# Shared experts as a loop with four scattered tiles per sequence, and the last three sequences in the head of the next stage

## The reference, cut to what matters

```
x = x + norm(attention(norm(x)))
x = x + norm(moe0(norm(x)))      # 16 experts, inner width 176, top 2, and shared experts of inner width 352
x = x + norm(ssm(norm(x)))       # a state space scan
x = x + norm(moe1(norm(x)))      # 16 experts, inner width 128, top 8, and shared ones of 256
```

```
y = sum over the two: w_e * ((silu(t @ w1[e].T) * (t @ w3[e].T)) @ w2[e].T)
z = (silu(t @ sw1.T) * (t @ sw3.T)) @ sw2.T      # the shared experts, for every token
moe0 = y + z
```

## Time and profile before

| | |
|---|---|
| median of 3 runs | 1998.63 us |
| profiled execution | 1997.82 us, its span 1996.1 us |
| PE busy | 1867.9 us, 94% of the span |
| PEld busy | 1413.5 us, 71% |
| DVE busy | 1270.9 us, 64% |
| ACT busy | 763.9 us, 38% |
| POOL busy | 426.5 us, 21% |
| mean granted clock | 0.959 |

### The profile page before, as it was taken

How to read it: one execution, slowest core, us unless ns; L and a number is a source line. 1 busy time by engine, 2 the same in 40 slices (tenths; PEclk the granted TensorE clock), 3 DMA queues, 4 the chain that set the end, 5 groups by cost and what they waited for, 6 DMA issues and landing times.

```text
span 1996.1 us, 34048 instructions
## 1 busy us (share of the span) xinstructions
PE 1867.9 (94%) x10114; PEld 1413.5 (71%) x10115; DVE 1270.9 (64%) x3685; ACT 763.9 (38%) x1479; POOL 426.5 (21%) x712
## 2 busy tenths in 40 slices
PE   5999999979989999568999999999999999999998
PEld 3566666557766666346888788888878887888787
DVE  3677776536422222387777877787787778877743
ACT  1566666632223333242343333334333433433321
POOL 1243444323744444200110011001001100110000
PEclk8999999979989999677999999999999999999999
DMA  9900000001322323411101110110111011101110
GB/s 359 211 4 1 0 0 1 1 1 64 116 93 93 95 92 95 184 35 59 59 6 64 62 61 5 64 58 19 51 64 59 6 64 59 54 15 48 43 48 11
DMA packets 75230, 121.03 MB, mean 61 GB/s; under 512 B 18164, under 2 KB 59252, under 8 KB 74612
## 3 DMA queue, kind: packets, MB, share of 16 engines
q1 hardware_dynamic: 68212, 100.92, 15.9%
q0 software_dynamic: 6912, 18.92, 2.7%
HBM read 81.73 MB, written 38.08 MB: 60 GB/s over the span
## 4 chain that ended last, share of the span: by engine, by line
PE 42%; issue 39%; DVE 9%; POOL 7%; ACT 2%; DMA 1%; DVEq 0%; SPq 0%; POOLq 0%; ACTq 0%
PE bank L599 5%; PE bank L184 5%; PE bank L1151 4%; PE bank L620 4%; PE bank L1216 3%; POOL sorted_in L822 2%; PE bank L1109 2%; PE bank L193 2%; PE bank L1157 2%; PE bank L1139 2%; PE bank L1244 2%; PE bank L610 1%; PE bank L528 1%; PE bank L1704 1%; DVE comb_got L2089 1%
## 5 line engine op out<-in xcount | busy, mean ns | idle before, releaser
L184 PE MATMUL bank<-moe_xT,up_w 128*128 128x256 f32 x2304 | 552.3, 383 | 0.0
L184 PEld LDWEIGHTS bank<-moe_xT,up_w 128*128 128x128 f32 x2304 | 433.9, 190 | 69.7 <-issue 11.4
L227 ACT ACTIVATE moe_silu<-bank 128x256 f32<-128x256 f32 x288 | 110.7, 384 | 609.2 <-PE bank L184 609.2
L193 PE MATMUL bank<-down_w,moe_hT 128*128 128x256 f32 x1152 | 305.4, 388 | 3.6 <-ACT moe_y L230 2.1
L193 PEld LDWEIGHTS bank<-down_w,moe_hT 128*128 128x128 f32 x1152 | 206.0, 190 | 37.9 <-issue 7.6
L1390 DVE TENSOR_REDUCE q_slots<-bank 128x4 f32<-128x1024 f32 (+1 forms) x96 | 117.7, 1226 | 77.0 <-PE bank L1151 76.4
L1298 ACT ACTIVATE probs<-bank 128x1024 f32<-128x1024 f32 x96 | 98.2, 1023 | 99.4 <-PE bank L1157 99.4
L599 PE MATMUL bank<-up_w,moe_xT 128*128 x320 | 116.7, 488 | 0.7 <-ACT moe_xT L663 0.6
L794 DVE TENSOR_TENSOR moe_h<-moe_silu,bank 128x176 f32<-128x176 f32 x80 | 27.0, 338 | 138.6 <-issue 86.2
L326 POOL TENSOR_TENSOR moe_prstd<-moe_pmv,minus_half 128x2 f32<-128x2 f32 x16 | 11.0, 690 | 484.4 <-DVE moe_pmv L304 484.4
L1151 PE MATMUL bank<-kT,qT 16*128 16x256 f32 (+1 forms) x1024 | 114.4, 351 | 0.0
(11 more groups left out here) (296 smaller groups left out, 3233.0 us busy)
## 6 DMA issues: line engine op xcount, KB each, us to landing
up_w<-comb_rows SPq DMA_DIRECT2D x32, 768.0 KB, 5.3
comb_got<-results SPq DMA_DIRECT2D x16, 768.0 KB, 7.8
moe_rows<-sorted_in SPq DMA_DIRECT2D x80, 128.5 KB
sorted_in<-zero SPq DMA_DIRECT2D x10, 1024.0 KB, 10.3
down_w<-comb_rows SPq DMA_DIRECT2D x16, 512.0 KB, 7.2
up_w<-in_up SPq DMA_DIRECT2D x2, 3168.0 KB, 15.3
up_w<-in_up SPq DMA_DIRECT2D x2, 2304.0 KB, 11.9
results<-moe_s_y SPq DMA_DIRECT2D x16, 256.0 KB
```

Source lines behind the costliest of these rows:

```text
L184: last = mm(k.bank[:, UP_BANK + i % 3, half * S:(half + 1) * S], m.w_up[:, c, at + half * m.inter:at + (half + 1) * m.inter], m.xT[:, par, ...
L193: last = mm(k.bank[:, SUM_BANK, j * D:(j + 1) * D], m.hT[:, i % 3, j * P:(j + 1) * P], m.w_down[:, m.expert(i), :], start=(i == 0 and j == ...
L227: nc.scalar.activation(m.silu[:, i % 3, :], k.bank[:, UP_BANK + i % 3, 0:S], ACT.Silu).then_inc(m.silu_ready, 1)
```

## The change

Three parts, by the code alone:

1. `SharedSteps` takes the place of `shared_steps`. It has 13 sequences (`EARLY`): five in the head, three turns of two in a loop, two in the rest. Sequences 4 to 11 carry four `scatter` steps each, two behind the first chunk and one behind each other (`PAIR_ROWS` = 4 buffers of pairs). `choose` 14 comes last but for one `down`.
2. POOL's scatter takes the places straight from DVE's tile; its copy and its spare add are gone. POOL's list is not a loop: 32 calls in a row.
3. Sequences 13, 14 and 15 of the shared experts (`Late`) come in the head of the fused loop, with the tiles and banks of moe1 (bank 7 for the transpose and for `down`, banks 4 to 6 for `up`) and one y buffer. `l_end`, behind period 0, waits for their stores.

```diff
-CHOICE = {..., (4, 0): (14,)}
+CHOICE = {...}
+PAIR_ROWS = 4
+EARLY = 13
+LAST_CHOICE = 14
...
+class SharedSteps:
+    def __init__(self, chunks):
+        self.chunks = chunks
+        self.turns = (EARLY - 3 - SCATTERS_FROM) // 2
+    def sequence(self, t, par, scatters, last):
+        ready = 0
+        for c in range(self.chunks):
+            yield "up", t, par, c
+            if c == 0 and (not isinstance(t, int) or t > 0):
+                yield "down", t - 1, (par - 1) % 2, 0
...
+            if c == 0 and not last:
+                yield "norm", t + 1, (par + 1) % 2, 0
+            if c == 1 and not last:
+                yield "turn_x", t + 1, (par + 1) % 2, 0
...
+            while scatters and ready < -(-PAIR_ROWS * (c + 1) // self.chunks):
+                yield "scatter", (t - SCATTERS_FROM) * PAIR_ROWS + ready, 0, ready
+                ready += 1
...
+    def rest(self):
+        yield from self.sequence(EARLY - 2, (EARLY - 2) % 2, True, False)
+        yield from self.sequence(EARLY - 1, (EARLY - 1) % 2, False, True)
+        yield "choose", LAST_CHOICE, 0, 0
+        yield "down", EARLY - 1, (EARLY - 1) % 2, 0
...
         if what == "scatter":
-            par = t % 2
-            if begun(t - 1):
-                dve.wait_ge(m.scattered[par], (t - par) * 16)
+            if begun(t - c):
+                dve.wait_ge(m.scattered[c], 8 * (t - c))
             for j in range(2):
-                normalise(m.pairs[:, par, j, 0:D], t)
+                normalise(m.pairs[:, c, j, 0:D], t)
...
-            pool.wait_ge(m.rows_ready, t + 1)
-            chain.link(g.tensor_copy(m.place[:, 2 * par:2 * par + 2], cols(m.places, t, 2)))
-            g.tensor_tensor(k.pool_spare[:, 0:1], k.minus_half[:, 0:1], k.minus_half[:, 0:1], ALU.add)
...
+    def scatter(t):
+        row = t % PAIR_ROWS
+        pool.wait_ge(m.rows_ready, t + 1)
+        for j in range(2):
+            at = bass.IndirectOffsetOnAxis(m.places[:, 2 * t + j:2 * t + j + 1], 0)
+            g.indirect_dma_start(m.sorted_in, at, m.pairs[:, row, j, :], None).then_inc(m.scattered[row], 16)
+    for t in range(TILES):
+        scatter(t)
...
+def late_tensor(k, m, pe):
...
+        if what == "l_turn":
+            pe.wait_ge(s.xn_ready, t + 1)
+            pe.wait_ge(s.y_read, t)
...
+        if what == "l_up":
+            w, lo = s.wide(c), E * 2 * s.inter + c * P
+            pe.wait_ge(s.xT_ready, m.turns + n + 1)
+            if n > 0:
+                pe.wait_ge(s.h_ready, m.up(t - 1, c) + 1)
...
+        if what == "l_down":
+            pe.wait_ge(s.h_ready, m.up(t + 1, 0))
...
+def late_scalar(k, m, act):
...
+        if what == "l_down":
+            act.wait_ge(s.y_full, m.turns + n + 1)
+            if n > 0:
+                act.wait_ge(s.stored[(t - 1) % 2], 16 * ((t - 1) // 2 + 1))
+            nc.scalar.copy(moe.y[:].rearrange("p j d -> p (j d)"), k.bank[:, SUM_BANK, :]).then_inc(s.y_read, 1)
...
     def head(self):
+        a, b, c = range(EARLY, B)
+        yield "c_fetch", 0, 0, 0
+        for what, t, i in (("l_norm", a, 0), ("l_turn", a, 0), ("l_up", a, 0), ("c_sum", 0, 0), ("l_up", a, 1), ("c_sum", 0, 1),
+                           ("l_up", a, 2), ("l_h", a, 0), ("c_norm", 0, 0), ("l_h", a, 1), ("c_fetch", 1, 0),
+                           ("experts", 0, 0), ("norm", 0, 0), ("l_h", a, 2), ("l_norm", b, 0), ("norm", 0, 1),
+                           ("l_down", a, 0), ("turn_x", 0, 0), ("l_turn", b, 0), ("feat", 0, 0), ("l_up", b, 0), ("feat", 0, 1),
+                           ("l_h", b, 0), ("l_up", b, 1), ("bcdt", 0, 0), ("l_h", b, 1), ("l_up", b, 2), ("turn_dt", 0, 0),
+                           ("dt", 0, 0), ("table", 0, 0), ("conv", 0, 0), ("one_plus", 0, 0), ("l_h", b, 2), ("table", 0, 1),
+                           ("dt", 0, 1), ("conv", 0, 1), ("l_norm", c, 0), ("dt", 0, 2), ("table", 0, 2), ("l_down", b, 0),
+                           ("gate", 0, 0), ("conv", 0, 2), ("l_turn", c, 0), ("gate", 0, 1), ("conv", 0, 3), ("l_up", c, 0),
+                           ("silu", 0, 0), ("l_up", c, 1), ("c_sum", 1, 0), ("l_h", c, 0), ("l_up", c, 2), ("c_sum", 1, 1),
+                           ("l_h", c, 1), ("c_norm", 1, 0), ("turn_c", 0, 0), ("turn_c", 0, 1), ("l_h", c, 2),
+                           ("norm", 1, 0), ("norm", 1, 1), ("turn_x", 1, 0), ("l_down", c, 0), ("dt", 0, 3), ("turn_dA", 0, 0),
+                           ("xdt", 0, 0)):
+            yield what, t, t % 2, i
+        yield from self.period(0, 0)
+        yield "l_end", B, 0, 0
+        yield from self.period(1, 1)
```

More of the change, by code:

```diff
@@ L388 @@
 CHOICE = {(0, 0): (0,), (0, 1): (1,), (0, 2): (2, 3), (1, 0): (4, 5), (1, 1): (6,), (1, 2): (7,), (2, 1): (8,), (2, 2): (9, 10),
-          (3, 0): (11,), (3, 1): (12,), (3, 2): (13,), (4, 0): (14,)}
+          (3, 0): (11,), (3, 1): (12,), (3, 2): (13,)}
 RANKS = {2: 0, 3: 1}
 SCATTERS_FROM = 4
[L394 to L415, removed]
+PAIR_ROWS = 4
@@ L529, in turn, with shared @@
         last.then_inc(done, 1)
-    def shared(what, t, c):
+    def shared(what, t, par, c):
         if what == "turn_x":
@@ L565, in shared @@
                              stop=True).then_inc(m.ranks_full, 1)
[L567 to L570 removed]
+    go_through(m.shared, pe, shared)
+    pe.wait_ge(m.y_read, EARLY)
     pe.wait_ge(m.table_ready, 1)
@@ L652, in shared @@
             nc.scalar.activation(m.score, m.score, ACT.Exp).then_inc(m.exp_ready, 1)
-    for what in shared_steps(m.shared_chunks):
-        shared(*what)
+    go_through(m.shared, act, shared)
     def block(what, b, row):
@@ new lines, in late_vector, with step @@
+def late_vector(k, m, dve):
+    s, moe = m.sparse, m.moe
+    def step(what, t, par, c):
+        n = t - EARLY
+        if what == "l_norm":
+            if n > 0:
+                dve.wait_ge(s.xT_full, m.turns + n)
+            for j in range(SEQ_TILES):
+                last = normalised(k, moe.xn[:, j, :], SEQ_TILES * t + j)
+            last.then_inc(s.xn_ready, 1)
+        if what == "l_h":
+            w = s.wide(c)
+            dve.wait_ge(s.silu_ready, m.up(t, c) + 1)
+            if n > 0:
+                dve.wait_ge(s.y_full, m.turns + n)
+            k.nc.vector.tensor_tensor(moe.hT[0:w, c, :], moe.silu[0:w, c, :], k.bank[0:w, UP_BANK + c, S:2 * S],
+                                      ALU.mult).then_inc(s.h_ready, 1)
+    return step
@@ L873, with late_sync, step @@
+def late_sync(k, m, sp):
+    s, moe = m.sparse, m.moe
+    def step(what, t, par, c):
+        if what == "l_down":
+            sp.wait_ge(s.y_read, t + 1)
+            sp.dma_start(s.shared_rows(t), moe.y[:]).then_inc(s.stored[t % 2], 16)
+        if what == "l_end":
+            for stored in s.stored:
+                sp.wait_ge(stored, 16 * B // 2)
+    return step
 HEADS, KV = 16, 4
@@ L2196, in head @@
[L2196 to L2199, removed]
-        for what, i in (("norm", 0), ("norm", 1), ("turn_x", 0)):
-            yield what, 1, 1, i
-        for what in ("dt", "turn_dA", "xdt"):
-            yield what, 0, 0, 3 if what == "dt" else 0
-        for t in (0, 1):
-            yield from self.period(t, t % 2)
+        a, b, c = range(EARLY, B)
+        yield "c_fetch", 0, 0, 0
```

162 lines of the change are left out of this document (105 added, 57 removed).

## The result

The change makes the kernel slower, by less than 1%: 2015.01 us (median of 9 runs, 2004.32 to 2020.05) against 1998.63 (9 runs, 1994.6 to 2004.96), ratio 1.0071, 95% interval 1.0049 to 1.0093. The forecast was 1986.5, and its range ended at 1998. Single times of either kernel spread over 10 to 16 us, so I compare stages within the profiled executions first, and times by their ratios.

The account below looks back on a forecast made before the run. TensorE, busy 94% of the span, was taken as the bound. Span 1996.1 - 22.5 (shared stage) + 11 (fused loop's head) = 1984.6 us; with the offset to measured time, 1986.5 us; range 1978 to 1998.

Parts of the forecast that it names:

- POOL's pace: Shared stage: a tile's two indirect DMAs take 2.56 us instead of 2.92, so 32 tiles take 82 us.
- wait price of 0.03: Shared stage: 0.03 us more per tile for waiting directly ahead of an indirect DMA, lowering the gain from 23.4 to 22.5 us.
- POOL no faster: Rival, shared stage: the gap between waiting DMAs stays as long as with copy and add; gain 11.9, time 1997.7; chance 0.13.
- The sum of the stage: Shared stage: three sequences fewer and quicker POOL tiles bring the first fetch of sorted rows earlier, -22.5 us.
- Clock through the scatter loop at 1.00: Shared stage: TensorE's clock stays 1.00 despite one gap of about 1.8 us in 10.
- Scatter loop loses clock: Rival, shared stage: TensorE at half clock needs 17 us a sequence; two such cost 10 us, time 1997; chance 0.04.
- Head +11: Head of the fused loop: three late sequences delay the first dab by 11 us, own spread +8 to +18.
- Cold head: Rival, fused loop's head: clock stays at 1.2 GHz from 826 on, head costs +34 us, time 2009.6; chance 0.06.
- hidden head: Rival, fused loop's head: late steps cost only DVE's and ACT's additions, 4 us or less, time 1979.5; chance 0.13.
- store behind the expert loads: Rival, fused loop's head: first late store lands about 6 us late, holding ACT's second y copy; time 1992; chance 0.08.
- Steady part: Fused loop after the first dab: equal time to the end in both kernels, difference 0.
- the upper end of the head: Fused loop's head: with the clock at half throughout, the first dab comes at 902.5 instead of 868.2, +34 us.

Follow-up runs that it names:

- e2_straight: Changed kernel with the shared experts' stage written out straight, without the loop, on TensorE, ACT, DVE and SP; 2010.93 us, ratio 1.0049.
- e12: e2_straight with indirect DMAs writing 256 of 257 columns (1,024 bytes a row) to a tensor of their own, experts' part left out; 1989.81 us, ratio 0.9942.
- e10: e2_straight with indirect DMAs writing 64 of 257 columns (256 bytes a row) to a tensor of their own, experts' part left out; 1989.38 us, ratio 0.9940.
- e13: e2_straight with indirect DMAs writing 128 of 257 columns (512 bytes a row) to a tensor of their own, experts' part left out; 1990.58 us, ratio 0.9958.
- e1: Changed kernel with POOL's offset copy and spare add put back ahead of each tile's two indirect DMAs, loop kept; 2006.34 us, ratio 1.0032.
- e4: Changed kernel with POOL's copy and spare add put back and the shared stage written out straight; 2003.37 us, ratio 1.0016.
- e5: e2_straight with POOL's 64 indirect DMAs replaced by 64 plain ones from SP to consecutive rows, experts' result wrong; 1979.0 us, ratio 0.9893.
- e14: e2_straight with POOL's 64 indirect DMAs replaced by 64 plain ones from POOL itself to consecutive places, experts' result wrong; 1979.2 us, ratio 0.9899.
- e9: e2_straight with two small POOL copies behind every indirect DMA, spacing the same 64 DMAs at 2.0 us; 2038.74 us, ratio 1.0191.

## Why the prediction was wrong, point by point

- **POOL's pace**: right inside a row of DMAs, 2.53 us a tile against 2.56; no wait price of 0.03 showed, and *POOL no faster* falls. But the 64 DMAs took 101.1 us (481.62 to 582.70) and not 82, as POOL ran dry five times.
- **"The loops of PE, ACT, DVE and SP (three turns of two sequences) and their register arithmetic cost nothing here: PE has 10.24 - 8.39 = 1.85 us to spare in each sequence."** This is the step that failed, though not by the loops, which cost nothing that e2_straight could show. It took for granted that TensorE, ACT and DVE keep their 8.39 us cadence whatever POOL's closer DMAs do. They don't: 46.2 us of late signals used up that room and 25.2 us beyond it, the restarts at half clock among them: the stage took 152.8 us and not 127.6. DVE, held up behind ACT, then let POOL run dry. What links POOL's DMAs to TensorE's signals stays open (last section).
- **The sum of the stage without that**: right, and for the reason given, as POOL's row ends last (564.7, first fetch at 566.28 in e12). e10, e12 and e13 keep loopless after's work and pace and only shrink the scattered rows: 126.9 to 127.3 us against 127.6 forecast (150.1 - 22.5). Their times, 1989.4 to 1990.6, are 3 to 4 us above the forecast 1986.5 and inside its range.
- **Clock through the scatter loop at 1.00**: wrong as measured (0.52 at 496 to 500), but as a result of the late signals. With the spare gaps and no lateness it held: 1.00 in e12 from 480 to 560 with PE busy 72 of 80 us. *Scatter loop loses clock* named a pause by POOL's pace as its cause; e12 has that pause and no loss. So the loss that this rival named came, by another cause.
- **Head +11**: right, +9.8 (58.9 to 61.2 us in all kernels with the late head, 47.1 to 50.3 without). From the first DVE step of the late work to the first dab it is 54.0 us (829.80 to 883.82), 55 forecast. Its steps, as time from the loop's first fetch; rows of after that answer to the earlier trace rows:

```profile
837.13 0.73 DVE L2239 TENSOR_SCALAR comb_got<-comb_got,comb_mv,comb_rstd 128x256 f32<-128x256 f32 x2
844.05 0.60 PE L1830 MATMUL bank<-ident,ssm_xn 128*128 128x128 f32 x4
855.31 0.17 DVE L2049 TENSOR_TENSOR s_u<-bank,dt_bias 128x16 f32<-128x16 f32 x1 [1.88 <-PE bank L1855]
870.67 1.00 DVE L2227 SCALAR_TENSOR_TENSOR comb_got<-comb_got,moe_weight 128x256 f32<-128x256 f32 x2
883.82 0.39 PE L1903 MATMUL bank<-dAT,sel 24*128 24x256 bf16 x2 [0.72 <-ACT dAT L1983]
```

  c_norm 13.4 (forecast 13.4), turn_x 20.3 (20.3), dt(0) 31.6 (32.4), the second half of c_sum(1) 46.9 (49.5), first dab 60.1 (61.3). The clock rose inside the first three chunks as said: 0.50 in 832 to 836, 0.81 to 840, 1.00 to 856, then 0.70 to 861. Of the 2.6 us at c_sum(1), 0.8 were gained by dt(0); the other 1.8 are as much as the forecast had put there for a second loss of clock. The clock did fall there (0.70), so why it cost nothing up to c_sum(1) is not shown; the first dab is only 1.2 us early. *Cold head* and *hidden head* both fall; so does *store behind the expert loads*, as ACT copied the second y at 863.57 with no idle time before it.
- **ACT_TABLE_LOAD**: the load at 855.58 took 1.28 us and the activation began at 856.87. The drain of 1.4 us that the Trainium skill (ScalarE: Activation LUTs, section What ACT_TABLE_LOAD costs) adds does not show.
- **Steady part**: 1.5 us longer, TensorE idle 1.04 us in [930.13, 995.64]; small against the spread; its cause is open.
- **Two sums** are slightly off, and nothing hangs on them: the upper end of the head (826.5 + 54 + 21.5) is 902.0 and not 902.5, and *POOL no faster* adds 2.5 us to its span where the forecast adds 1.9.
- **The missing rival** was one that couples engines without a shared buffer. Nothing in the trace of before showed it, as that has no late signal. But I had costed a pause between two of POOL's DMAs as pure loss, and never asked what a closer row of them does to others.

## What to carry to other kernels

When an engine waits and its input has long been computed, compare the producer's end with the consumer's start: here a gap of microseconds labelled "remote" was a late signal of the core's own TensorE, and the cause lay in a third engine. Before speeding up a row of indirect DMAs, look at the size of a row and try one of 1,024 or 512 bytes; here the pauses between larger ones, a copy and a spare add of 0.2 us each and a wait for a buffer, were worth more than they cost in the stage. And price a moved step at both ends: the 9.8 us in the head would have been repaid by a stage 23 us shorter, but not by one 7 us shorter, as in e1 and e4 (142.7 and 143.5 us) with the pauses back.

## What the runs showed of the hardware

- TensorE's semaphore increments let ACT start up to 10.4 us after the matmul's end in after (568.20 to 578.64) while POOL issued indirect DMAs of 128 rows over 1,024 bytes each 1.265 us; of three in a row each was some 3.6 us behind the last (494.70, 498.18, 501.90). In the five rows of DMAs that end in a wait of POOL, ACT's last resumption came 1.6 to 2.7 us behind the end of the last DMA (499.55 and 501.90 in the first).
- In these runs it came only with three things together: rows over 1,024 bytes (or not a power of two, or packets over 4,096 bytes; the runs don't part these), indirect addressing, and a period near 1.3 to 1.5 us. Not enough are the same rows by plain DMAs (e5, e14), the same DMAs at 2.0 us (e9), or 1,024 bytes at 1.265 us (e12). Near 1.46 us it also depends on the buffers: 0 to 8.1 us with two, 25.9 to 43.2 with four.
- By what path a row's size reaches TensorE's signals no run tells. In both e2 and e12 a packet of the scatter carries four rows and takes 181 ns on average, so the traffic in the trace shows no difference; this stays open.
